# Householder reflections of a 512x512 eigendecomposition: the order of a reflection's steps and the engines they run on

## The reference

```python
deg = jnp.sum(A, axis=0) + jnp.sum(A, axis=1) - jnp.diagonal(A)
L_norm = d_inv_sqrt[:, None] * (jnp.diag(deg) - A) * d_inv_sqrt[None, :]
_, U = jnp.linalg.eigh(L_norm)
agg = jnp.einsum('mn,bnd->bmd', U.T, features)
out = jax.nn.relu(agg @ W1 + b1) @ W2 + b2
return jnp.einsum('nm,bmd->bnd', U, out)
```

## Time and profile before

| | |
|---|---|
| median of 3 runs | 4845.44 us (4843.95 to 4860.02) |
| profiled execution | 4845.71 us, span 4843.9 us |
| mean granted TensorE clock | 0.816 |
| busy share of the span | PE 63%, DVE 67%, ACT 22%, POOL 9% |
| chain that ended last | DVE 54%, PE 38%, issue 4% |
| L1114, L1115 (ScalarE scalings) | 510 each, mean 297 and 283 ns |
| L1106 (ScalarE evictions of tiles) | 144, median 575 ns |
| L1283 `jk` (dot product of two vectors) and its read | 1530 each, mean 154 to 156 and 83 ns |
| L929 (GpSimd product, 1 to 4 elements) | 510, mean 197 ns |

### The profile page before, as it was taken

How to read it: one execution, slowest core, us unless ns; L and a number is a source line. 1 busy time by engine, 2 the same in 40 slices (tenths; PEclk the granted TensorE clock), 3 DMA queues, 4 the chain that set the end, 5 groups by cost and what they waited for, 6 DMA issues and landing times.

```text
span 4843.9 us, 67935 instructions
## 1 busy us (share of the span) xinstructions
PE 3070.8 (63%) x19024; PEld 1606.0 (33%) x19024; DVE 3240.5 (67%) x20663; ACT 1064.4 (22%) x4245; POOL 427.3 (9%) x1829
## 2 busy tenths in 40 slices
PE   3887777777777878888850010000165767599998
PEld 1554444444444434443320000000043523244433
DVE  6777777888878888888887889999822213102323
ACT  0212222222222223222210000000013122314532
POOL 0000000000000010010012221111000000000000
PEclk7888999899989989999975555555587988689998
DMA  2000000000000000000000000000000000000000
GB/s 88 2 1 1 2 1 1 1 2 1 2 1 2 1 2 1 2 1 1 1 1 0 0 0 0 0 0 0 0 0 0 17 0 0 0 0 0 0 0 35
DMA packets 3094, 20.89 MB, mean 4 GB/s; under 512 B 432, under 2 KB 560, under 8 KB 1072
## 3 DMA queue, kind: packets, MB, share of 16 engines
q1 hardware_dynamic: 2736, 16.85, 0.9%
HBM read 12.66 MB, written 4.19 MB: 3 GB/s over the span
## 4 chain that ended last, share of the span: by engine, by line
DVE 54%; PE 38%; issue 4%; ACT 2%; POOL 1%; DMA 0%; DVEq 0%; SPq 0%; POOLq 0%; ACTq 0%
PE ps L610 7%; PE ps L879 6%; DVE H L1670 5%; DVE jq L1283 4%; PE ps L614 3%; DVE C L1462 2%; PE ps L886 2%; DVE tsc L1446 2%; DVE WG L1403 2%; DVE H L1283 2%; DVE tsc L1456 2%; DVE tsc L1436 2%; PE ps L851 2%; PE ps L602 2%; DVE TMP L1398 2%
## 5 line engine op out<-in xcount | busy, mean ns | idle before, releaser
L619 PE MATMUL ps<-dots,ones 128*128 128x3 f32 x1020 | 202.6, 269 | 366.1 <-DVE dots L1283 365.3
L610 PE MATMUL ps<-C 128*32 128x131 f32 (+39 forms) x10200 | 383.9, 282 | 76.3 <-DVE C L1462 23.2
L610 PEld LDWEIGHTS ps<-C 128*32 128x32 f32 x10200 | 260.4, 116 | 463.1 <-DVE C L1462 386.9
L619 PEld LDWEIGHTS ps<-dots,ones 128*128 128x128 f32 x1020 | 164.4, 201 | 727.4 <-DVE dots L1283 726.3
L1114 ACT ACTIVATE sz<-C,tsc 128x4 f32<-128x4 f32 (+3 forms) x510 | 151.7, 297 | 1022.4 <-DVE tsc L1453 1022.4
L602 PE MATMUL ps<-eye,same 128*128 128x512 f32 x518 | 327.1, 717 | 0.0
L569 PE MATMUL ps<-WK,LT 128*128 128x512 f32 x512 | 301.0, 671 | 0.0
L929 POOL TENSOR_TENSOR xm<-C,WK 128x4 f32<-128x4 f32 (+3 forms) x510 | 100.7, 197 | 2265.4 <-DVE C L1462 1921.6
L569 PE MATMUL ps<-C,LT 128*128 128x512 f32 x512 | 298.0, 665 | 0.0
L879 PE MATMUL ps<-C,V 128*128 128x512 f32 (+1 forms) x504 | 287.5, 727 | 8.5 <-issue 7.5
L1112 ACT ACTIVATE tsc<-tsc 128x1 f32<-128x1 f32 x510 | 103.4, 203 | 761.0 <-DVE tsc L1416 761.0
(11 more groups left out here) (468 smaller groups left out, 7262.0 us busy)
## 6 DMA issues: line engine op xcount, KB each, us to landing
out_x<-X SPq DMA_DIRECT2D x4, 1024.0 KB, 3.8
...
```

The costliest lines, as they stand in the source:

```text
L610: mm(ps[q * QUAD:(q + 1) * QUAD, 0, 0:c + n], SI[:, b, 0, 2 * j:2 * j + 1].broadcast_to([P, QUAD]), AS[:, b, q, k * QUAD:P + n], start=(b ...
L619: mm(ps[:, 3, 0:3], ones[:], dots[:], start=True, stop=True).then_inc(S["dots_ps"], 1)
```

## The change

- **Pivot element ahead of the rows.** TensorE makes x1 by a product with e ahead of the row products, into the same bank. The coefficients of the pivot row are a product of their own (`pivot_row`), made for reflection r + 1 behind the dots and `pause(r, 1)` of reflection r, after z and u of r.
- **y by one summation.** One product of the rows with `pick` for all blocks and one of the corrections of y, written side by side, and one `tensor_reduce` over both.
- **Pivot column in the rows' shadow.** g for r + 1 is one `tensor_tensor_reduce` for each block (`pivot_column`), behind the `SO` column of r, before VectorE waits for the rows of r + 1.
- **Unit-vector dots on TensorE.** e.y and e.g come from one product of e, spread over 128 columns, with y and g; only x.y is summed through `dots`.
- **z and u on GpSimd.** Two instructions after mu: y, g, x and e lie side by side in `XYEG`, so one product with mu and one subtraction make both. GpSimd also copies x into `XYEG`.
- ScalarE evicts side work ahead of the scalings and stores both scalars at once (`ES`, unpacked by two copies at the end).
- `plan_gaps` lets a piece start one gap earlier after an eviction and evicts at `g // 2 + 2`; the last piece is now seen in reflection 426. `keep_clock` runs only after that (`EULER_END`).
- A mask `above` (minus `below`) is made once by GpSimd; it takes the sign of sn, which is gone.

```diff
 class Gaps:
-            g = max([self.gap] + [2 * self.seen[n] for n in needs])
+            g = max([self.gap] + [2 * self.seen[n] - 1 for n in needs])
-        return self.at(key, g // 2 + 1 if g % 2 == 0 else g // 2 + 2)
+        return self.at(key, g // 2 + 2)
...
+EULER_END = max(PLAN.seen.values())
...
                 if piece is None:
-                    keep_clock(HEAT[r // P][h])
+                    if r > EULER_END:
+                        pe.wait_ge(S["eu_sb"], 4 * TILES)
+                        keep_clock(HEAT[r // P][h])
...
                 pe.wait_ge(S["x_ready"], r)
+                pe.wait_ge(S["e_ready"], r)
+                mm(ps[:, 0, c + n:c + n + 1], spread(XYEG[:, r % 2], k, 2), SI[:, k, 0, 2 * j:2 * j + 1], ...)
+                if r > 1:
+                    pe.wait_ge(S["zu_ready"], r - 1)
                 for b in range(k, KB):
                     for q in range(QUADS):
...
+                m.then_inc(S["row_ps"], 1)
                 pause(r, 0)
-                mm(ps[:, 1, c:c + n], spread(E, k, j % 2), SI[:, k, 0, 0:n], ...)
-                mm(ps[:, 3, 0:3], ones[:], dots[:], ...)
+                pe.wait_ge(S["y_ready"], r)
+                pe.wait_ge(S["g_ready"], r)
+                mm(ps[:, 1, 1:3], spread(XYEG[:, r % 2], k, 2), XYEG[:, r % 2, k, 1:4:2], ...)
+                pe.wait_ge(S["dots_in"], r)
+                mm(ps[:, 3, 0:1], ones[:], dots[:], ...)
                 pause(r, 1)
+                if (r + 1) % PANEL > 0 and r + 1 < N - 1:
+                    pivot_row(r + 1)
+            def pivot_row(r):
+                    pe.wait_ge(S["zu_ready"], r - 1)
+                pe.wait_ge(S["e_ready"], r)
+                mm(ps[:, 2, 0:2 * j], spread(XYEG[:, r % 2], k, 2), SI[:, k, 0, 0:2 * j], ...)
...
+                g_.tensor_tensor(xm[...], SI[:, k:KB, 0, 2 * j:2 * j + 1], above[:, k:KB, r:r + 1], ALU.mult)
+                g_.tensor_copy(after[:, :, 2:3], eye[:, k:KB, r + 1:r + 2])
+                go(g_.tensor_copy(this[:, :, 0:1], SI[:, k:KB, 0, 2 * j:2 * j + 1]))
+                for t_ in PLAN.pool[r]:
+                    add_into_x(t_)
+                pool.wait_ge(S["beta_ready"], r)
+                pool.wait_ge(S["g_ready"], r)
+                step(g_.tensor_scalar(step2[:, k:KB, :], this[:, :, 2:4], tsc[:, 7:8], None, ALU.mult))
+                g_.tensor_tensor(uz4, step2..., this[:, :, 0:2]..., ALU.subtract).then_inc(S["zu_ready"], 1)
...
+                dve.wait_ge(S["row_ps"], r)
                 ts_(nsq, n2, 1e-33, None, ALU.add).then_inc(S["norm_ready"], 1)
+                m_prod = ch.mark(tt(terms[:, :, 0:QUAD], ps[:, 0, 0:c]..., pick..., ALU.mult))
+                    m_prod = ch.mark(tt(terms[:, :, QUAD:QUAD + n], SO[:, k:KB, 0:n], ps[:, 0, c:c + n]..., ALU.mult))
                 go(ts_(sg, x1, 0.0, -0.5, ALU.is_lt, ALU.add))
+                v.tensor_reduce(y, terms, AX.X, ALU.add).then_inc(S["y_ready"], 1)
                 m_rc = ch.mark(v.reciprocal(rc, root))
+                ttr(jk[:, k:KB], x, y, dots[:, 0:1]).then_inc(S["dots_in"], 1)
                 m_c1 = ch.mark(stt(c1, rc, nsq, root, ALU.mult, ALU.add))
+                tt(mu, c1, sg, ALU.mult).then_inc(S["beta_ready"], 1)
                 m_un = ch.mark(stt(un, x1, mu, mu, ALU.subtract, ALU.mult))
+                v.reciprocal(tsc[:, 8:10], tsc[:, 6:8]).then_inc(S["scale_ready"], 1)
+                dve.wait_ge(S["pivot_ps"], r)
+                m_tz = ch.mark(stt(tz, mu, g1, y1, ALU.mult, ALU.subtract))
                 dve.wait_ge(S["dots_ps"], r)
                 m_uy = ch.mark(stt(uy, mu, y1, xy, ALU.mult, ALU.subtract))
+                m_yb = ch.mark(stt(yb, y, nu, mask, ALU.mult, ALU.mult))
+                m_cc = ch.mark(ts_(cc, uy, ns, nu, ALU.mult, ALU.mult))
                 m = stt(next4, four(xb), cc, four(yb), ALU.mult, ALU.add)
...
+                stt(column(SO, k, 2 * j), x, k2, szv, ALU.mult, ALU.add).then_inc(S["so_done"], 1)
+                if not last and r + 1 < N - 1:
+                    pivot_column(r + 1)
+            def pivot_column(r):
+                a = AS[:, :, r % P // QUAD, r // P * QUAD + r % QUAD]
...
+                dve.wait_ge(S["so_done"], r - 1)
+                dve.wait_ge(S["g_ps"], pivots(r))
+                for b in range(k, KB):
+                    m = ttr(jq[:, b, 0:2 * j], SO[:, b, 0:2 * j], ps[:, 2, 0:2 * j], XYEG[:, r % 2, b, 3:4], init=a[:, b:b + 1])
```

More of the change, by code:

```diff
@@ L613, in reflect @@
[L613 to L620 removed]
+                        m = mm(ps[q * QUAD:(q + 1) * QUAD, 0, 0:c + n],
+                               SI[:, b, 0, 2 * j:2 * j + 1].broadcast_to([P, QUAD]), AS[:, b, q, k * QUAD:P + n],
+                               start=(b == k), stop=(b == KB - 1), skip_group_check=True)
@@ new lines, in reflect @@
+                m.then_inc(S["row_ps"], 1)
+                pause(r, 0)
+                pe.wait_ge(S["y_ready"], r)
+                pe.wait_ge(S["g_ready"], r)
+                mm(ps[:, 1, 1:3], spread(XYEG[:, r % 2], k, 2), XYEG[:, r % 2, k, 1:4:2], start=True, stop=True).then_inc(S["pivot_ps"], 1)
+                pe.wait_ge(S["dots_in"], r)
+                mm(ps[:, 3, 0:1], ones[:], dots[:], start=True, stop=True).then_inc(S["dots_ps"], 1)
+                pause(r, 1)
+                if (r + 1) % PANEL > 0 and r + 1 < N - 1:
+                    pivot_row(r + 1)
@@ L1400, in reduced, with reflect @@
-            def reduced(out, vecs, k):
-                nv, nb = len(vecs), KB - k
-                return v.tensor_reduce(WG[:, 0:nv * nb].rearrange("p (v b) -> p v b", v=nv), out, AX.X, ALU.add)
-            def reflect(p, r, j, k, prev):
-                nb, c, last = KB - k, (KB - k) * QUAD, j == PANEL - 1 and p < PANELS - 1
-                x, z, u4, z4, next4 = SI[:, k:KB, 0, 2 * j], SI[:, k:KB, 0, 2 * j + 1], *(SI[:, k:KB, :, 2 * j + n] for n in range(3))
-                e, a, mask = column(E, k, r % 2), a_column(k, r), column(below, k, r)
-                y, g, xb, yb, szv = yv[:, k:KB], gv[:, k:KB], xm[:, k:KB], ymn[:, k:KB], sz[:, k:KB]
-                n2, x1 = ps[:, 0, c + 2 * j:c + 2 * j + 1], ps[:, 1, c + 2 * j:c + 2 * j + 1]
-                xy, y1, g1 = ps[:, 3, 0:1], ps[:, 3, 1:2], ps[:, 3, 2:3]
-                root, nsq, sg, rc, c1, un, mu, ns, nu, sn, uy, cc, k2, tz, uz = (
-                    tsc[:, n:n + 1] for n in (1, 2, 3, 4, 5, 6, 7, 8, 9, 11, 12, 13, 14, 15, 10))
-                dve.wait_ge(S["coef_ps"], r)
+            def reflect(p, r, j, k):
+                nb, c, n, last = KB - k, (KB - k) * QUAD, 2 * j, j == PANEL - 1 and p < PANELS - 1
+                x, next4, mask = SI[:, k:KB, 0, 2 * j], SI[:, k:KB, :, 2 * j + 2], column(below, k, r)
+                y, xb, yb, szv = XYEG[:, r % 2, k:KB, 1], xm[:, k:KB], ymn[:, k:KB], sz[:, k:KB]
+                n2, x1 = ps[:, 0, c + n:c + n + 1], ps[:, 0, c + n + 1:c + n + 2]
+                xy, y1, g1 = ps[:, 3, 0:1], ps[:, 1, 1:2], ps[:, 1, 2:3]
+                root, nsq, sg, rc, c1, un, mu, ns, nu, uy, cc, k2, tz, uz = (
+                    tsc[:, i:i + 1] for i in (1, 2, 3, 4, 5, 6, 7, 8, 9, 12, 13, 14, 15, 10))
+                terms = TMP[:, 0:nb * (QUAD + n)].rearrange("p (b c) -> p b c", b=nb)
+                dve.wait_ge(S["row_ps"], r)
@@ L1422, in reflect @@
                 go(ts_(sg, x1, 0.0, -0.5, ALU.is_lt, ALU.add))
[L1423 to L1425 removed]
+                ch.need(m_prod)
+                v.tensor_reduce(y, terms, AX.X, ALU.add).then_inc(S["y_ready"], 1)
                 dve.wait_ge(S["root_ready"], r)
                 m_rc = ch.mark(v.reciprocal(rc, root))
[L1428 to L1433 removed]
@@ L1440, in reflect @@
-                ttr(jk[:, 2, k:KB], e, g, dots[:, 2:3]).then_inc(S["dots_in"], 1)
                 if r > 1:
@@ L1508, in _ @@
             ch.wait()
-            dve.wait_ge(S["coef_ps"], N - 1)
-            out, m = corrections(PANEL - 1, (1,), KB - 1)
-            step(m)
-            step(reduced(out, (1,), KB - 1))
-            step(tt(gv[:, KB - 1:KB], a_column(KB - 1, N - 1), WG[:, 0:1], ALU.add))
-            tt(dots[:, 0:1], gv[:, KB - 1:KB], E[:, KB - 1, 1:2], ALU.mult).then_inc(S["dots_in"], 1)
+            dve.wait_ge(S["coef_ps"], 1)
+            dve.wait_ge(S["so_done"], N - 2)
+            step(tt(TMP[:, 0:NS - 2], SO[:, KB - 1, 0:NS - 2], ps[:, 1, QUAD:QUAD + NS - 2], ALU.mult))
+            step(v.tensor_reduce(tsc[:, 10:11], TMP[:, 0:NS - 2], AX.X, ALU.add))
+            step(tt(XYEG[:, 1, KB - 1, 3:4], a_column(KB - 1, N - 1), tsc[:, 10:11], ALU.add))
+            tt(dots[:, 0:1], XYEG[:, 1, KB - 1, 3:4], XYEG[:, 1, KB - 1, 2:3], ALU.mult).then_inc(S["dots_in"], 1)
             dve.wait_ge(S["saved"], N - 2)
-            go(ts_(erow_s[:, N - 2:N - 1], ps[:, 1, QUAD + NS - 2:QUAD + NS - 1], -1.0, None, ALU.mult))
+            go(ts_(ES[:, N - 2, 0:1], ps[:, 1, QUAD + NS - 2:QUAD + NS - 1], -1.0, None, ALU.mult))
             dve.wait_ge(S["dots_ps"], N - 1)
@@ L1520, in _ @@
             ch.wait()
```

(2 more changed lines are left out.)

154 lines of the change are left out of this document (72 added, 82 removed).

## The result

| | before | after |
|---|---|---|
| median | 4849.9 us (4 runs) | 4890.0 us (4885.1 to 4896.3, 4 runs) |
| ratio to before | | 1.008, interval 1.0061 to 1.0098 |
| span of the profiled execution | 4843.9 us | 4894.5 us |
| mean granted TensorE clock | 0.816 | 0.766 |

The account below looks back on a forecast made before the run. The 510 reflections were taken as a loop of VectorE and TensorE waiting for each other. Shorter turns gave -149 us and paid-back costs +64, so -85 from 4845.4: forecast 4760 us, range 4640 to 4875.

Parts of the forecast that it names:

- What is paid back: Costs set against the -149 us gain: lower clock, additions into X and the ends, together +64 us.
- (a): Turns at the lower clock after panel updates: two more small matmuls lengthen each by 0.9 us, 1.4 turns a panel, +40.
- (b): Gaps without a piece up to reflection 426 lose the keep-alive, 88 of 849 empty: +10 us (0 to 40).
- (c): 16 GpSimd additions of a block to X hold up VectorE's L1473, which the pivot column now follows: +12 us (0 to 18).
- (d): Two 128x512 copies at the end and strided memsets: +2 us.
- Rival 2: Clock: busier TensorE leaves the lower level sooner, (a) and (b) unpaid, 4645 us; chance 0.13.
- y by one summation and mu to the next x: VectorE's half of a turn with 4 blocks: gains of 0.63 and 0.04 us, 2.82 instead of 3.49.
- The sum at the upper clock: Turn changes of -0.75, -0.35, -0.11 and +0.04 us with 4 to 1 blocks, over all reflections -149 us.
- Rival 1: GpSimd's z and u block VectorE in every turn, up to 0.24 us each: 4908 us at full price; chance 0.10.

Follow-up runs that it names:

- b_small: Kernel before the change with two more 2-column products in each turn, as many as the change adds: 4951.7 us, 1.0194.
- k_zu_vector: Changed kernel with keep-alive back and 256-column fillers at panel updates, but z and u on VectorE again: 4891.1 us, 1.0092.
- k_top: Changed kernel with keep-alive back, 256-column fillers at panel updates and 256 columns more in gaps with two transposes: 4704.0 us, 0.9697.
- b_top: Kernel before the change with 256-column fillers at panel updates and 256 columns more in gaps with two transposes: 4808.6 us, 0.9895.

## Why the prediction was wrong

**The step that failed is "What is paid back", terms (a) and (b).** The forecast said that the clock falls a little more often and priced it at 40 + 10 us. By the runs it is the largest term of the case, and larger than the gain.

- (b), the missing keep-alive: forecast +10 (0 to 40). Measured 71 us in the new order, 43 us in the old. The empty gaps were counted rightly, 88 of them, and each of the three runs of 14 reflections lies at the lower clock nearly as a whole, 65 to 85 us. But the cost is not there: 67 of the 71 us lie in the first 50 reflections, where the other 34 gaps are empty, and which the forecast gave no thought of its own. The +10 leans to a clock that mostly holds; no row said so, and the upper end of the term, 40, was too low as well.
- (a), the turns after a panel update: forecast +40, from turns that are longer at the lower clock. It missed that they also stay at the lower clock **longer**: with 1 block 10 to 27 us instead of 7 to 10, with two small products more in each turn. The length of a single turn was even overpriced: 5.50 us with 1 block against 4.84, so +0.66, where 0.9 was forecast. b_small shows the longer stay by itself: 97 us for products that cost nothing at the upper clock. Why such small products have this effect the runs don't settle; they show that it comes with them and goes with a filler. Fillers bring it back: 81 us at the updates, 34 in the transposing gaps.
- (c), the additions into X: forecast +12, since with 4 blocks they were held to have lain in the shadow. Only one of the 16 turns with an addition has 4 blocks (reflection 126), and in none had it lain in the shadow whole: at the upper clock such a turn was 0.4 us over its stretch's median with 4 blocks, 0.5 to 0.8 with 3 and some 0.9 and 1.1 with 2 and 1. After the change it is 0.8 to 0.9 over it. That adds some 2 us for all 16 (estimate from these turns). (d), the ends: forecast +2, measured 7.
- Rival 2 had the sign wrong: "TensorE is busier in a turn and leaves the lower level sooner". Busy it was, 26.62 of 27 us, and it stayed there.

The Trainium skill, "TensorE: Matmul & The Clock Gate", section "What's actually happening", says that the array's clock is throttled by default and is released when TensorE has been at work. The fall in the emptied gaps agrees with that. The 27 us at 0.50 with TensorE's row full (26.62 us) don't: to be busy in the profile was not enough, and here the measurement decides.

**What held, by the same steps.**

- *y by one summation and mu to the next x:* 2.82 us forecast with 4 blocks, 2.85 measured; 0.36 for the sum forecast, 0.35 measured. Medians of the VectorE half at the upper clock 2.87, 2.74, 2.63 and 2.52 against 2.82, 2.72, 2.61 and 2.55 worked out.
- *Pivot element ahead of the rows:* -0.08 forecast, nothing measured. The product ahead costs 0.31 up to the rows' start (629.40 to 629.71), not 0.24, and the rows' own end is 0.07 before L1449.
- *Pivot column in the rows' shadow:* spacing 0.155 forecast, 0.15 measured (630.20 to 630.35). From x to L1449 1.33, 1.17 and 1.02 with 3, 2 and 1 blocks, against 1.31, 1.16 and 1.00. It costs what was said, and that is why the last two stretches gain nothing.
- *z and u on GpSimd:* hidden, as forecast. The pair ends 0.89 after mu starts. The part is worth 0.2 to 0.3 us a turn at the new order (k_zu_vector); from mu to the next x all the moves together bring 0.06 (1.34 to 1.28), where 0.04 was forecast.
- *The sum at the upper clock:* turns of 4.52, 4.08, 3.81 and 3.53 us against 5.16, 4.46, 3.90 and 3.51: -81, -49, -12 and +3 us, together -139; forecast -149.
- *Rival 1* (GpSimd holds VectorE up in each turn) is out. The second instruction of GpSimd and the one of VectorE that meets it:

```profile
L968 POOL TENSOR_TENSOR C<-step,XYEG 128x32 f32<-128x32 f32 x127 | 30.8, 243 | 10.6
...
L1479 DVE SCALAR_TENSOR_TENSOR ymn<-XYEG,tsc,WK 128x4 f32<-128x4 f32 x127 | 27.7, 218 | 0.0
```

L1479 has a mean of 218 ns, the length of its like before. In the turn above it starts at 633.06 while L968 runs (632.94 to 633.18), and isn't longer. That is so in 416 of the 510 turns, and the longest L1479 of all takes 221 ns. So the exclusion seen in the earlier trace rows didn't show here. Beside the long additions into X it is still there after the change: L1496, the successor of L1473, takes 1.13 to 1.19 us in 15 turns. Why the two cases differ wasn't tried.

The account: -139 at the upper clock, and 44 us more in the end between the first and the last x; the rest, some 183 us, is nearly all the lower clock's: 884 us of it instead of 385, in turns whose medians are 0.8 to 2 us longer there. Added up over the turns in which the clock was low at least in part, what lies above the upper clock's medians is 70 us before and 215 after; the 31 turns that hold a panel update take 286 us before and 313 after. With the clock held up in both orders the change is worth 97 to 105 us, not the 139. The traces of k_top and b_top differ by 119 us, b_top's being from the slowest of its runs. Turns at the lower clock cost the same in both (47 and 48 us above the medians), so the lower clock that is left isn't the difference. The additions into X aren't it either, nor are the ends (under 1 us between these two traces). The updates gain 2 us, where the 139 counts 8 for their turns; the rest is spread over the turns at the upper clock, and why stays open.
